# Rotated-heads stage of a decoder kernel written anew: sums of squares, projected means and mixing in small tiles of the matmul array

## Chip, cores and metric

One core of one Trainium2 chip (trn2) runs the whole program. The metric is the device time of one execution in microseconds (us), the median of the runs shown.

## What is computed

The program computes two decoder layers on x (32 items of 100 rows by 256) and a context of 361 rows by 192 per item. Each layer is attention, cross attention and a mixture of experts. The stage in question is the self attention of the second layer, "rotated heads":

```python
Q, K, V = (x @ w + b).reshape(Bn, Sn, 16, 16)        # heads of 16
prep = lambda t: tanh(t @ w1 + b1) @ w2 + b2          # 16 -> 256 -> 16, Q and K, every head
q1, k1 = complex(prep(Q)) @ H, complex(prep(K)) @ H   # 8 complex numbers of a head
qe, ke = real(R @ q1), real(R @ k1)                   # R works along the batch: items 0..7 alone are turned
qq, kk = sum(qe ** 2, -1), sum(ke ** 2, -1)           # (B, S, H)
s = qq[:, :, None, :] * kk[:, None, :, :]
attn = softmax(s / s, axis=2)                         # s / s is one wherever it is finite
out = (attn @ V) @ wo + bo
```

So the attention of a head is the mean of its values over the rows, times a factor that is one where s is finite. R mixes item a with item b = a + 1 for the first four pairs of items.

## The kernel before

`decoder` runs six stages one after another. `rotation_phase` (line 1916) is the fourth, and takes the items in 16 pairs. Pairs 0 to 3 (`TURNED`) are turned, the other twelve are plain. Each engine has its own program (`@block.tensor` and so on), an order written out by hand in its `run`, which is called once for each pair k. In it `before` is pair k-1, `after` k+1, `following` k+2, `third` k+3. I call one such call a step. All loops are unrolled, and engines meet by semaphores alone.

TensorE in a step: `first_layer` eight times (L2084: four matmuls of 32 rows, one in each row group of the array, 400 columns), `last_layer` four times (L2098: eight matmuls whose output has 32 partitions, in four column groups), `make_rows` (L2050, four transposes), `make_part` twice (L2057, keys and queries of the pair after), `make_mean` (L2065, values' mean of the pair after), `norms` twice (L2113: one matmul of 128x128 by 400 that writes each head's sum of squares on all its 16 partitions), `project` (L2119, four matmuls of 128x100 by 256), and, for turned pairs, `mix` twice (L2106 and L2108, real and imaginary part).

In PSUM (`g.psum`) six banks in three pairs hold first layers (`pair_banks`), one (`vec`) the last layers' output, and one (`side`) all else, in turn: rows, keys, queries, means, sums of squares, projection. So on `side` each product waits until the one ahead of it is copied out.

ScalarE takes tanh of two banks at a time (L2210, 16 in a step), copies rows, keys and queries (`keep_rows`, `keep_part`) and squares (L2215, L2218). VectorE normalises rows of the pairs to come (`combine`, `second_norm`, `stats`, `apply`), turns (`turn_by` L2337), finds the ends of the keys' sums (`ends_of_keys` L2343), and multiplies (`spans` L2350, `weigh` L2357 to L2364) on 128x400 elements. GpSimd gathers expert rows from DRAM (`gather`, L1976, four indirect DMAs for a pair), takes roots for the norms (L94, L96) and adds rows and bias (L1990 to L2003).

Just ahead of the stage TensorE is done with the stage before, and just behind it `wide_cross_phase` begins with a DMA.

## Time and profile before

| what | us |
|---|---|
| runs, median (lowest to highest) | 3473.21 (3470.78 to 3478.59) |
| profiled execution, its own time | 3493.37 |
| its span | 3491.2 |
| TensorE matmul busy, whole program | 3271.7 (94%) |
| VectorE, ScalarE, GpSimd busy | 1814.3, 1613.6, 1520.3 |
| stage in question, first gather to last addition | about 1229 to 1641 |

The profile is one execution. The time line gives start and length of each group of like instructions, and in square brackets how long the engine had been idle and who released it. A matmul in f32 shows as two MATMUL entries, so "x8" is four matmuls. In shapes such as 128*32, the weights have 128 rows and 32 columns. What a block of TensorE takes of its time is the distance from its start to the next block's start, since blocks overlap at their ends.

### The profile page before, as it was taken

The page shows a single profiled execution, that of the slowest core. Times are in us where ns is not written, and L with a number is a line of the kernel's source. Part 1 is how long each engine was busy: PE and PEld are TensorE (multiplying, and loading weights), DVE is VectorE, ACT ScalarE, POOL GpSimd, SP SyncE. Part 2 cuts the span into 40 slices and gives each one's busy share as a digit, 9 for nine tenths or more (in the row PEclk, how much of TensorE's full clock was granted, in tenths as well). Part 3 has the DMA queues.
Part 4 walks back from the last instruction along what each step waited for, and adds up shares of the span by engine and source line. Part 5 has one row for each costly group of instructions (what it writes and reads, how often), then busy time and mean ns, then how long its engine had stood idle before and what let it go on. Part 6 is the DMA issues. An engine that isn't in the chain of part 4 may idle for free. (4 is left out here: it accounts for less than half of the span.)

```text
span 3491.2 us, 70582 instructions
## 1 busy us (share of the span) xinstructions
PE 3271.7 (94%) x26268; PEld 2383.1 (68%) x26269; DVE 1814.3 (52%) x5671; ACT 1613.6 (46%) x3299; POOL 1520.3 (44%) x2061
## 2 busy tenths in 40 slices
PE   8997999988998869998999999999999999999997
PEld 6774566656776734443677777777777688999986
DVE  4665777755887545664444545454545465111123
ACT  4653666655764046775445554555555411111111
POOL 1002444434775154551566566666666554000035
PEclk9999999998998879999999999999999999999998
DMA  8501111100000630001000000000000013999952
GB/s 279 207 2 42 42 42 42 43 26 1 21 23 25 196 90 20 20 20 38 8 8 14 8 8 8 14 8 8 8 14 1 1 38 129 326 326 325 325 185 78
DMA packets 111486, 263.29 MB, mean 75 GB/s; under 512 B 24003, under 2 KB 70240, under 8 KB 95840
## 3 DMA queue, kind: packets, MB, share of 16 engines
q1 hardware_dynamic: 90208, 224.70, 20.1%
q0 software_dynamic: 16384, 26.29, 2.7%
q10 hardware_dynamic: 4608, 8.39, 0.6%
q8 instruction: 191, 3.13, 0.4%
q14 instruction: 95, 0.78, 0.1%
HBM read 196.61 MB, written 62.65 MB: 74 GB/s over the span
## 5 line engine op out<-in xcount | busy, mean ns | idle before, releaser
L2546 POOL TENSOR_SCALAR wide_probs<-wide_probs,wide_inverse 100x361 f32<-100x361 f32 x512 | 603.9, 1192 | 0.1
L2813 ACT ACTIVATE wide_probs<-wide_probs,wide_least 100x361 f32<-100x361 f32 x512 | 300.9, 592 | 8.6 <-DVE wide_least L2910 8.6
L2910 DVE CUSTOM_DVE_ANT_0 wide_probs<-banks,wide_bias 100x361 f32<-100x361 f32 x512 | 251.6, 529 | 45.1 <-issue 40.0
L2598 PE MATMUL banks<-w_wide_v,wide_c 64*120 64x512 f32 (+1 forms) x1152 | 266.4, 591 | 0.9 <-DVE wide_v L2896 0.9
L2592 PE MATMUL banks<-wide_c,w_wide_k 64*128 64x361 f32 x1536 | 257.4, 467 | 7.4 <-DMA wide_c<-in_ctxT 7.4
L2210 ACT ACTIVATE rot_h<-banks,w_rot_b 128x800 f32<-128x800 f32 x256 | 223.6, 924 | 86.2 <-PE banks L2084 81.1
L2544 POOL TENSOR_TENSOR wide_hold_pool<-eps 100x1 f32<-100x1 f32 x256 | 49.4, 193 | 455.1 <-DVE wide_inverse L2916 455.1
L3354 ACT ACTIVATE tiles_hT<-banks 128x512 f32<-128x512 f32 x114 | 68.1, 597 | 347.8 <-PE banks L3270 347.8
L3270 PEld LDWEIGHTS banks<-tiles_xT,tiles_w 128*128 128x128 f32 x1824 | 214.1, 193 | 4.5 <-issue 1.6
L2592 PEld LDWEIGHTS banks<-wide_c,w_wide_k 64*128 64x128 f32 x1536 | 150.5, 189 | 96.6 <-issue 10.5
L2625 PE MATMUL banks<-wide_kT,wide_qT 64*100 64x361 f32 x1024 | 208.4, 478 | 8.3 <-DVE wide_least L2910 6.6
L3270 PE MATMUL banks<-tiles_xT,tiles_w 128*128 128x128 f32 x1824 | 214.6, 276 | 1.2 <-DVE tiles_xT L3516 1.2
L3283 PE MATMUL banks<-tiles_w,tiles_hT 128*128 128x256 f32 x912 | 206.4, 379 | 0.3 <-issue 0.3
L3192 POOL TENSOR_TENSOR combine_hold<-eps 100x1 f32<-100x1 f32 x32 | 7.6, 236 | 442.0 <-DMA slots<-tiles_out 431.9
L2598 PEld LDWEIGHTS banks<-w_wide_v,wide_c 64*120 64x120 f32 (+1 forms) x1152 | 120.7, 180 | 107.1 <-issue 93.3
L3283 PEld LDWEIGHTS banks<-tiles_w,tiles_hT 128*128 128x128 f32 x912 | 168.8, 190 | 21.1 <-issue 0.4
L2643 PEld LDWEIGHTS banks<-ident,wide_probs 100*120 100x120 f32 (+1 forms) x1536 | 142.5, 140 | 31.2 <-issue 29.3
L2643 PE MATMUL banks<-ident,wide_probs 100*120 100x100 f32 (+1 forms) x1536 | 158.8, 254 | 3.0 <-ACT wide_probsT L2819 3.0
L2807 ACT COPY wide_v<-banks 120x512 f32<-120x512 f32 (+1 forms) x96 | 56.2, 585 | 223.7 <-PE banks L2598 223.7
L2804 ACT COPY wide_kT<-banks 128x361 f32<-128x361 f32 x128 | 59.0, 461 | 205.7 <-PE banks L2592 205.7
L2920 DVE COPY wide_probsT<-banks 121x400 f32<-121x400 f32 x128 | 72.9, 570 | 151.2 <-PE banks L2643 151.2
L2655 PE MATMUL banks<-wide_probsT,wide_v 120*64 120x100 f32 (+1 forms) x3072 | 148.9, 253 | 0.1
(469 smaller groups left out, 7378.6 us busy)
## 6 DMA issues: line engine op xcount, KB each, us to landing
tiles_w<-in_moe_w SPq DMA_DIRECT2D x114, 1024.0 KB, 5.1
slots<-zeros SPq DMA_DIRECT2D x58, 512.0 KB, 5.7
cross_c<-in_ctxT SPq DMA_DIRECT2D x32, 270.8 KB, 4.4
wide_c<-in_ctxT SPq DMA_DIRECT2D x32, 270.8 KB, 4.0
mix_kT<-slots SPq DMA_DIRECT2D x32, 256.0 KB, 4.2
slots<-mix_m_tiles_out ACTq DMA_DIRECT2D x32, 256.0 KB, 4.0
tiles_rows<-slots SPq DMA_DIRECT2D x57, 128.0 KB, 4.7
slots<-tiles_out SPq DMA_DIRECT2D x57, 128.0 KB, 4.9
```

The source lines that it names most:

```text
L2210: nc.scalar.activation(t.h[:, u % 2, m, 2 * half:2 * half + 2, :], pair_banks(i), ACT.Tanh, bias=w.b1[:, m:m + 1]).then_inc(h_done[i], 1)
L2546: last = nc.gpsimd.tensor_scalar(t.probs[:, i, j, :], t.probs[:, i, j, :], t.inverse[:, i, j:j + 1], None, ALU.mult)
L2592: last = nc.tensor.matmul(make_bank(unit, lane)[:, 0:CTX], w.k[rows_of(lane), k, at:at + P], t.c[rows_of(lane), of.buf, k, :], start=(k == ...
L2598: last = nc.tensor.matmul(make_bank(unit, lane)[0:kw, :], t.c[rows_of(lane), of.buf, k, k0:k0 + kw], w.v[rows_of(lane), k, of.hf * BANK:(o ...
L2625: last = nc.tensor.matmul(scores(j), t.qT[rows_of(j), here.hf, m, lane, :], t.kT[rows_of(j), here.hf, m, lane, :], start=True, stop=True)
L2643: last = nc.tensor.transpose(turned(bank)[0:cols, at], t.probs[:, i, j, k0:k0 + cols], g.ident[0:S, 0:S])
L2655: last = nc.tensor.matmul(out[rows_of(j), :], t.v[0:kw, of.hf, k, LANE_OF(i), at:at + WD], t.probsT[0:kw, group % STEP_GROUPS, bank, cols] ...
L2813: last = nc.scalar.activation(t.probs[:, i, j, :], t.probs[:, i, j, :], ACT.Exp, bias=t.least[:, i, j:j + 1], scale=-1.0, accum_out=t.rows ...
L2910: last = nc.vector.tensor_tensor_reduce(t.probs[:, i, j, :], scores(j), t.bias[:, :], -1.0, LARGEST, ALU.add, ALU.min, t.least[:, i, j:j + 1])
L2920: nc.vector.tensor_copy(t.probsT[:, group % STEP_GROUPS, 0, :], turned(0)[0:TMAX, 0:TURN_COLS]).then_inc(b[group].probsT_dve, 1)
L3270: last = nc.tensor.matmul(out_, t.w1[:, lane, c, m * P:(m + 1) * P], t.xT[:, lane, c, :], start=(c == 0), stop=(c == DC - 1))
L3283: last = nc.tensor.matmul(tile_out, t.hT[:, lane, m, :], t.w2[:, lane, m, :], start=(m == 0), stop=(m == HM - 1))
```

## The change

The whole of `rotation_phase` is written anew. `norms` makes four matmuls with 32 output partitions each, one for each lane (item of the pair) and half of the heads, in the four column groups of the array; each head then has 4 rows of 100, and VectorE works on 128x100 in place of 128x400. `mix` packs the eight real rows of each head, and makes matmuls with 64 output partitions. The mean of the values is spread over masked weights (`masked`) and projected ahead (`make_projected`, four matmuls with 32 output partitions by 256 columns, copied by VectorE to `rows`). `project` then multiplies the factors (`least`) with these rows: two matmuls of 64 rows, into two banks (`side`, `vec`) for plain pairs, or one behind the other for pairs 0 to 3. `headsT` and `mean_sum` are gone. The mean has columns 400 to 403 of `side` to itself. On GpSimd, gathers read `slot_i` itself, wait for no copy, and stand ahead of the additions; rows of pair 1 are added by VectorE. Tanh's table is loaded ahead of the first pair.

```diff
-                nc.tensor.matmul(side[:, 0:COLS], t.sum8[:, :], t.squares[:, part, :], start=True, stop=True).then_inc(ready, 1)
+                for lane in range(LANES):
+                    for c in range(DC):
+                        group = lane * DC + c
+                        last = nc.tensor.matmul(out[group * GROUP_ROWS:(group + 1) * GROUP_ROWS, :], sums(lane, c), rows(lane, c), start=True, stop=True)
...
-                nc.tensor.matmul(side[:, 0:COLS], t.real[:, :], t.by_cos[:, :], start=True, stop=False)
+                for c in range(DC):
+                    nc.tensor.matmul(side[c * MIXED:(c + 1) * MIXED, 0:LANES * S], t.real[:, :], by_chunk(t.by_cos)[:, c, :], start=True, stop=False)
...
+            def make_projected(p):
+                pe.wait_ge(s.masked, p + 1)
+                for group in range(LANES * DC):
+                    last = nc.tensor.matmul(rows_out[group * GROUP_ROWS:(group + 1) * GROUP_ROWS, :], t.masked[:, group, :, :].rearrange("p h r -> p (h r)"), w.proj[:, group % DC, :], start=True, stop=True)
...
-                for lane in range(LANES):
-                    for c in range(DC):
-                        last = nc.tensor.matmul(by_lane(side)[:, lane, :], t.headsT[:, c, lane, :], w.proj[:, c, :], start=(c == 0), stop=(c == DC - 1))
+                pe.wait_ge(s.ratio, p + 1)
+                pe.wait_ge(s.rows, p + 1)
+                half = P // LANES
+                if two_banks(p):
+                    for lane, out in ((0, side), (1, vec)):
+                        last = nc.tensor.matmul(out[0:S, 0:D], t.least[lane * half:(lane + 1) * half, :], t.rows[lane * half:(lane + 1) * half, :], start=True, stop=True)
+                    last.then_inc(s.proj_ready, 1)
+                else:
+                    nc.tensor.matmul(by_lane(side)[:, 0, :], t.least[0:half, :], t.rows[0:half, :], start=True, stop=True).then_inc(s.lane_ready, 1)
+                    pe.wait_ge(s.lane_ready, p + 1)
+                    nc.tensor.matmul(by_lane(side)[:, 1, :], t.least[half:P, :], t.rows[half:P, :], start=True, stop=True).then_inc(s.proj_ready, 1)
...
+                nc.vector.tensor_scalar(t.least[:, :], query_norms(p), t.k_least[:, :], None, ALU.mult)
+                nc.vector.tensor_scalar(t.most[:, :], query_norms(p), t.k_most[:, :], None, ALU.mult).then_inc(s.spans, 1)
```

TensorE, part of a plain step, from `project` of pair k-1 on, before:

```order
L2119 MATMUL banks<-w_rot_proj,rot_headsT 100x256 x4
L2098 MATMUL banks<-rot_h,rot_w 32x400 x8
L2084 MATMUL banks<-rot_q,rot_w 128x400 x4
L2065 MATMUL banks<-rot_ybar,w_rot_qkv 128x2 x4
L2084 MATMUL banks<-rot_q,rot_w 128x400 x4
L2113 MATMUL banks<-rot_squares,rot_sum 128x400
L2098 MATMUL banks<-rot_h,rot_w 32x400 x8
L2084 MATMUL banks<-rot_q,rot_w 128x400 x4
L2113 MATMUL banks<-rot_squares,rot_sum 128x400
```

TensorE, the like part now, from the second last layer on (L2122 is `make_projected`, L2131 `project`, L2115 `norms`, L2051 `make_part`):

```order
L2094 MATMUL banks<-rot_h,rot_w 32x400 x8
L2122 MATMUL banks<-w_rot_proj,rot_masked 32x256 x4
L2078 MATMUL banks<-rot_q,rot_w 128x400 x4
L2131 MATMUL banks<-rot_rows,rot_least 100x256 x2
L2078 MATMUL banks<-rot_q,rot_w 128x400 x4
L2094 MATMUL banks<-rot_h,rot_w 32x400 x8
L2115 MATMUL banks<-rot_squares,rot_sum 32x100 x4
L2078 MATMUL banks<-rot_q,rot_w 128x400 x4
L2051 MATMUL banks<-rot_yT,w_rot_qkv 128x200 x4
```

The blocks with 32 output partitions that are new stand right behind a last layer, which has the same shape of tile. The queries' product has moved to the place behind the keys' sums, and the mean's product, not shown, to the start of the step, a pair later than before.

GpSimd, one step before (roots of the two norms, bias, additions of rows, gathers):

```order
L96 TENSOR_TENSOR rot_ln_rstd<-rot_ln_vareps,neg_half 100x1
L2001 TENSOR_TENSOR rot_moe_seen<-eps 100x1
L2003 TENSOR_TENSOR x<-x,w_rot_proj_b 100x256 x2
L1990 TENSOR_TENSOR rot_moe_sum<-rot_moe_sum,w_mix_ln_w 100x256 x2
L1993 TENSOR_TENSOR rot_moe_sum<-rot_moe_sum,w_mix_ln_b 100x256 x2
L1997 TENSOR_TENSOR x<-x,rot_moe_sum 100x256 x2
L1973 TENSOR_TENSOR rot_moe_hold<-eps 100x1
L1976 DMA rot_moe_got<-slots,rot_gather_i 100x256 x4
```

And now:

```order
L96 TENSOR_TENSOR rot_ln_rstd<-rot_ln_vareps,neg_half 100x1
L1978 DMA rot_moe_got<-slots,mix_slot_i 100x256 x4
L1988 TENSOR_TENSOR rot_moe_sum<-rot_moe_sum,w_mix_ln_w 100x256 x2
L1991 TENSOR_TENSOR rot_moe_sum<-rot_moe_sum,w_mix_ln_b 100x256 x2
L1994 TENSOR_TENSOR x<-x,rot_moe_sum 100x256 x2
L94 TENSOR_TENSOR rot_ln_vareps<-rot_ln_meanvar,eps 100x1
L96 TENSOR_TENSOR rot_ln_rstd<-rot_ln_vareps,neg_half 100x1
```

The gathers have moved ahead of the additions, between the roots of the one norm and those of the other, and both norms of a pair are now done in one step.

## Rows read from the trace of the kernel before

**Rows 1.** The page, busy time by engine, whole program

```profile
PE 3271.7 (94%) x26268; PEld 2383.1 (68%) x26269; DVE 1814.3 (52%) x5671; ACT 1613.6 (46%) x3299; POOL 1520.3 (44%) x2061
```

**Rows 2.** Windows: steps 2, 4, 5 to 14, and last step with its tail

```profile
core 0: us, PE busy (x) PEld busy (x) DVE busy (x) ACT busy (x) POOL busy (x), PEclk, DMA share, GB/s
...
1312.77:1339.69 26.92, 24.62 (x184) 12.04 (x180) 15.64 (x37) 16.62 (x23) 12.92 (x23) 1.00 0.06 15
...
1366.63:1391.27 24.64, 23.01 (x178) 11.02 (x174) 14.56 (x36) 16.34 (x23) 11.26 (x21) 1.00 0.04 11
1391.27:1610.56 219.29, 214.49 (x1684) 100.39 (x1680) 132.26 (x309) 168.23 (x231) 118.07 (x203) 1.00 0.07 18
1610.56:1641.00 30.44, 20.64 (x146) 8.05 (x138) 13.98 (x20) 12.51 (x16) 0.00 (x0) 0.89 0.00 1
```

**Rows 3.** Time line of TensorE in a plain step: start, length, line, tiles

```profile
1572.72 0.95 PE L2084 MATMUL banks<-rot_q,rot_w 32*128 32x400 f32 x8
1573.61 1.62 PE L2057 MATMUL banks<-rot_yT,w_rot_qkv 128*128 128x200 f32 x8
...
1580.94 1.97 PE L2119 MATMUL banks<-w_rot_proj,rot_headsT 128*100 128x256 f32 x8
1582.84 1.55 PE L2098 MATMUL banks<-rot_h,rot_w 128*32 128x400 f32 x16
1584.33 0.95 PE L2084 MATMUL banks<-rot_q,rot_w 32*128 32x400 f32 x8
...
1587.27 0.94 PE L2113 MATMUL banks<-rot_squares,rot_sum 128*128 128x400 f32 x2
1588.14 1.55 PE L2098 MATMUL banks<-rot_h,rot_w 128*32 128x400 f32 x16
```

**Rows 4.** Time line of TensorE in a turned step: mixing and its waits

```profile
1315.48 0.91 PE L2106 MATMUL banks<-rot_by_cos,rot_real 128*128 128x400 f32 x2 [0.88 <-DVE rot_by_sin L2337]
...
1317.66 0.94 PE L2113 MATMUL banks<-rot_squares,rot_sum 128*128 128x400 f32 x2 [0.59 <-ACT rot_squares L2215]
```

**Rows 5.** Time line of TensorE, self attention: 16 small matmuls, then next block

```profile
130.76 0.88 PE L274 MATMUL banks<-self_probsT,self_v 100*17 100x100 f32 x32
131.57 1.62 PE L218 MATMUL banks<-self_yT,w_self_qkv 128*128 128x200 f32 x8
```

**Rows 6.** Groups by line, whole program: matmuls with 64 output partitions

```profile
L2655 PE MATMUL banks<-wide_probsT,wide_v 120*64 120x100 f32 x2048 | 132.9, 250 | 0.0
```

**Rows 7.** Groups by line, plain steps: busy us, mean ns, then idle before

```profile
L1976 POOL DMA_INDIRECT rot_moe_got<-slots,rot_gather_i x34 | 35.0, 1031 | 9.4 <-issue 9.4
L96 POOL TENSOR_TENSOR rot_ln_rstd<-rot_ln_vareps,neg_half 100x1 f32<-100x1 f32 x38 | 22.2, 584 | 3.0
L1997 POOL TENSOR_TENSOR x<-x,rot_moe_sum 100x256 f32<-100x256 f32 x18 | 12.6, 722 | 0.0
L2304 DVE SCALAR_TENSOR_TENSOR rot_moe_sum<-rot_moe_got,mix_coef,mix_x 100x256 f32<-100x256 f32 x18 | 7.9, 478 | 0.0
L2357 DVE RECIPROCAL rot_inverse<-rot_least 128x400 f32<-128x400 f32 x10 | 26.4, 2645 | 0.0
```

**Rows 8.** Time line of TensorE at the stage's start

```profile
1261.78 1.72 PE L2084 MATMUL banks<-rot_q,rot_w 32*128 32x400 f32 x8 [1.11 <-ACT rot_h L2210]
...
1269.08 0.95 PE L2084 MATMUL banks<-rot_q,rot_w 32*128 32x400 f32 x8
...
1286.72 0.95 PE L2084 MATMUL banks<-rot_q,rot_w 32*128 32x400 f32 x8
```

**Rows 9.** Time line of the last step and its tail

```profile
1611.44 0.95 PE L2084 MATMUL banks<-rot_q,rot_w 32*128 32x400 f32 x8
...
1631.88 2.65 DVE L2357 RECIPROCAL rot_inverse<-rot_least 128x400 f32<-128x400 f32 x1
...
1636.51 3.70 PE L2119 MATMUL banks<-w_rot_proj,rot_headsT 128*100 128x256 f32 x8 [5.76 <-DVE rot_headsT L2364]
1640.25 0.75 DVE L2371 TENSOR_TENSOR x<-x,banks 100x256 f32<-100x256 f32 x2 [3.89 <-PE banks L2119]
```

More of the change, by code:

```diff
@@ L2101, in last_layer @@
                     last.then_inc(vectors_ready[part], 1)
-            def mix(pr, part):
-                pe.wait_ge(turned[part], pr[2])
-                nc.tensor.matmul(side[:, 0:COLS], t.real[:, :], t.by_cos[:, :], start=True, stop=False)
-                for lane in range(LANES):
-                    last = nc.tensor.matmul(by_both(side)[:, :, lane, :], t.imag[:, :], by_both(t.by_sin)[:, :, 1 - lane, :], start=False, stop=(lane == LANES - 1))
-                last.then_inc(mixed_ready[part], 1)
@@ L2183, in _ @@
+            make_rows(0)
+            make_part(0, 1, s.k_ready)
+            first_layer(0, 0)
+            make_part(0, 0, s.q_ready)
+            first_layer(0, 1)
+            for k in range(PAIRS):
+                step(k)
+            pe.wait_ge(s.rows, PAIRS)
+            norms(LAST_PAIR, 0, query_norms(LAST_PAIR), s.qn_ready)
             pe.wait_ge(s.spans, PAIRS)
-            project(LAST)
+            project(LAST_PAIR)
         @block.scalar
@@ L2243, in _ @@
-            keep_part(FIRST, 1, s.k_ready, s.k_kept)
-            keep_part(FIRST, 0, s.q_ready, s.q_kept)
-            for k in range(2):
-                tanh(FIRST, k)
-            pairs(act, run)
+                if not is_turned(k):
+                    square(k, 0)
+            keep_rows(0)
+            keep_part(0, 1, s.k_ready, s.k_kept)
+            tanh(0, 0)
+            keep_part(0, 0, s.q_ready, s.q_kept)
+            tanh(0, 1)
+            for k in range(PAIRS):
+                step(k)
@@ new lines, in step @@
+            def step(k):
+                before, after, following = k - 1, k + 1, k + 2
+                late = not two_banks(before)
+                if is_turned(before):
+                    turn_by(before, 0)
+                if before >= 0 and is_pair(following):
+                    combine(following)
+                if before >= 0:
+                    keep_mean(before)
+                if is_pair(after):
+                    add_rows_up(after)
+                if before >= 0 and not is_turned(before):
@@ L2408, in _ @@
-            for lane, b, n in FIRST[3]:
-                dve.wait_ge(s.out_shifted, n)
-                nc.vector.tensor_tensor(g.x[:, b, :], g.x[:, b, :], v.sum[:, 0, lane, :], ALU.add).then_inc(s.stored, 1)
-            stats(FIRST)
-            copy_slots(THIRD)
-            apply(FIRST)
-            combine(SECOND)
-            add_rows_up(FIRST)
-            second_norm(SECOND)
-            keep_mean(FIRST)
-            pairs(dve, run)
-            if LAST[4]:
-                turn_by(LAST, 0)
@@ new lines, in step @@
+                if before >= 0 and not late:
+                    add(before)
+                if not is_turned(k):
+                    ends_of_keys(k)
+                if is_pair(following):
+                    stats(following)
+                if before >= 0 and late:
+                    add(before)
+                if is_pair(following):
+                    apply(following)
+                if is_turned(k):
+                    ends_of_keys(k)
+            combine(0)
+            second_norm(0)
@@ L2431 @@
+            add_rows(0)
+            stats(0)
+            combine(1)
+            apply(0)
+            second_norm(1)
+            add_rows(1)
+            add_rows_up(0)
+            stats(1)
+            apply(1)
+            for k in range(PAIRS):
+                step(k)
+            keep_mean(LAST_PAIR)
+            keep_projected(LAST_PAIR)
+            spans(LAST_PAIR)
+            weigh(LAST_PAIR)
+            add(LAST_PAIR)
 WIDE_TILES = [(0, 121), (121, 120), (241, 120)]
```

577 lines of the change are left out of this document (305 added, 272 removed).

## The prediction

> **What bounds the kernel now.** I read the page first: TensorE's matmuls are busy 94% of the span, the other engines half of it [rows 1]. So what a change in this stage is worth is read from TensorE. Then the windows, one for each kind of step. Steps 5 to 14 (plain pair behind plain pair) take 219.29 us, 21.93 each, and TensorE is busy for 214.49 of them: 0.48 us idle in a step. A turned step takes 26.92 with 2.3 idle, step 4 takes 24.64, the last one with its tail some 30 [rows 2]. ScalarE is busy 168.23 of the 219.29, 16.8 a step. It and VectorE bind only where a wait falls badly. Then the time line, for the price of each block as the distance to the next start: first layer 0.89, keys or queries 1.62 with the overlap at the end, `project` 1.90, last layer 1.49, `norms` 0.87 [rows 3]. The granted clock is 1.00, the higher level, in all these steps.
>
> **Prices of the new blocks.** None of them is in the trace, so I draw a line through blocks that use the array in tiles. A last layer is eight matmuls over four column groups, four passes of 400 columns one behind the other in a group (each f32 matmul is two entries): 1600 columns in 1.49 us. A first layer is 800 columns in 0.89 [rows 3]. So a column costs (1.49-0.89)/800 = 0.75 ns and a block 0.29 us beside. The 16 small matmuls of the self attention are eight passes of 100 columns in a group, 800 columns in 0.81 us [rows 5], where the line says 0.89; this shows that small tiles in one bank do run side by side. I take 0.24 for the fixed part, between 0.21 and 0.29.
> - `norms`: four column groups, two passes of 100: 0.15+0.24 = 0.39, for 0.87.
> - `make_projected`: two passes of 256: 0.38+0.24 = 0.63. New.
> - `project` of plain pairs: two row groups, two banks, again two passes of 256: 0.63, for 1.90. For pairs 0 to 3 one lane waits for the other: 2 x 0.55 = 1.1.
> - `mix`: two column groups. An entry of 64 output partitions by 100 columns costs 132.9/2048 = 0.065 us [rows 6]; eight of these and four of double length make 1.04, say 1.1. Before it was 1317.66-1315.48-0.59 = 1.59 [rows 4].
>
> Bounds: the least is the slope alone, 0.15, 0.38 and 0.38. The most is one tile after another at the full-array rate (0.24 us for 256 columns by `project`'s row, and not under 0.12 for a short one, half of that): `norms` 0.98, `make_projected` 1.90, `project` 1.1, `mix` 1.8. The values taken lie near the lower end because rows 5 is the nearest shape by far.
>
> Here a rule of the Trainium skill speaks against small tiles (TensorEngine Tiling, Key Properties): a change of tiling mode drains the engine. If that drain is the fixed part, `norms` and `make_projected` of a plain step, all directly behind a last layer with the same tile shape, would pay nothing, and the three would cost 0.68 and not 1.41. The trace has no two unlike blocks of one mode in a row, so it does not decide; my sum charges the fixed part everywhere.
>
> **A plain step.** Removed: 2 x 0.87 + 1.90 = 3.64. Added: 2 x 0.39 + 0.63 + 0.63 = 2.04. TensorE's work falls from 21.45 to 19.85 us. Waits: what must come back from VectorE in time is each a short hop. I set the blocks one behind another by these prices. Behind the queries' sums VectorE has one first layer's time (0.89) for two products of 100 columns; behind `make_projected` the copy has 0.89; behind the keys' sums the two ends have 0.89. Each hop needs some 0.55 to 0.65 beyond the block's end, so 0.3 is spare. The tanh behind `project` comes 0.5 us late, since TensorE now does less between two first layers. With 0.1 more elsewhere the idle time is 0.6, for 0.48. So a step takes 20.45, and **ten steps give 10 x 1.5 = 15 us**. VectorE's savings (the reciprocal of 2.65 us [rows 7] becomes a quarter of that) are off the path here. ScalarE at 16.8 in 20.4 is no bound.
>
> **Turned steps.** In steps 2 and 3 removed work is 3.64 + 2 x 1.59 = 6.8, added 0.78+0.63+1.1+2.2 = 4.7. Of 2.3 us idle [rows 2], which were TensorE waiting for VectorE's turning and ScalarE's squares [rows 4], nearly all goes, as a first layer or more stands now between. 26.9 becomes 22.5: 2 x 4.4 = 8.8, I take 8.6. Step 4 has one mix of the two: 24.64 becomes 21.6, 3.0.
>
> **The start.** GpSimd issues gathers 0.9 us sooner (it waits for no copy), but VectorE now combines pair 1 ahead of normalising pair 0, so rows reach TensorE some 1.6 us later. The first tanh then comes sooner, between keys and queries and with its table loaded, which wins 1.3 back. I book 0.3 as lost at the first projected step. Step 0 took 1286.72-1261.78 = 24.9 [rows 8]. By the sum of blocks it is 19.9, to which I add 3 for the lower clock (a first layer entry took 1.72 us there and 0.95 from 1269.08 on [rows 8]): 2.1 less than before. Step 1 is where time is lost. VectorE combines pair 2 only when the rows of pair 1 are out, and the keys' ends of pair 0 stand behind stats and apply of pair 2. That chain is 0.5 + 2.7 (combine, statistics) + 1.6 (GpSimd's roots: 2 x 0.58 and small ones) + 5.2 (four gathers, (35.0+9.4)/34 = 1.31 each) + 4.2 (additions, 6 x 0.70) + 1.0 + 1.9 + 0.8 = 17.9 us [rows 7]. It begins 2.4 us behind the start of these rows' transposes (their copy waits for two tanh) and so ends at 20.3; TensorE has 15.2 us of blocks in that time (six first layers, three last layers, keys, queries, one mix, `norms`, transposes) and stands idle some 5 us at the start of step 1. So that step is 27.2 (0.3 more than before). A stop of this length may also lower the clock. Behind the 5.76 us stop of the tail `project` took 3.70, not 1.97 [rows 9, 3]. I add 2.0, some 4 us of blocks at half speed, between 0 and 8 (the whole of step 1 low would be about 10).
> Sum to step 4: 0.3 - 2.1 + 0.3 + 2.0 - 8.6 - 3.0 = **-11.1**.
>
> **The tail.** From the last step's first layer at 1611.44 to the last addition at 1641.0 it is 29.6 us [rows 9]. The last step itself loses 1.5 as others do, and the reciprocal and three more full-width products on the critical path, some 4.4, become about 1.3. `project` falls from 3.70 to 0.6 to 1.3, but the pair's mean and `make_projected` (1.8) are added. I come to 23: **-6.5**. The next stage begins with a DMA and has the same idle time ahead of it.
>
> **The sum.** -15 - 11.1 - 6.5 = -32.6, call it 33: the profiled execution would go from 3493.4 to 3460. It lies 20 us over the median of the runs; the same 33 off the median, 3473.2, gives **3440**. A measurement of this kernel tells about 0.2%, 7 us, from no change.
>
> **Rivals.**
> - Cheaper joins: the fixed part is not paid behind a last layer. Three blocks of a plain step save 0.24 each; over 16 pairs about 11 us: 3429. For it: the self attention's block lies 0.08 under the line. Against: no like pair of blocks. This is what the drain rule would give.
> - Late hops: the spare 0.3 us behind sums, copy or ends is not there, since VectorE's small operations have a floor that the 400-wide rows do not show. With one miss of 1.2 us in each plain step and some in the turned ones, 15 are given back: 3455.
> - The clock stays low after the stop in step 1, or falls again, and pairs 1 to 2 run at half speed: 9 more, 3449.
> - GpSimd's chain: with gathers ahead of additions, the loop from combine to the next combine is 2.7+1.6+5.2+4.2+1.0+1.6+0.5 = 16.8, under 20.4. Only if it grows past that (gathers at 2.2 us each) does it bind; then the gain is about nothing: 3472.
> - Slower: small tiles whose output lies in one bank run one after another. Then `norms`, `make_projected` and `project` take 4.96 for the 3.64 removed; plain steps lose 0.9 to 1.3, turned ones gain nothing, the stop stays, the tail gains little: about +9, 3482. It decides from the point where the four blocks take more than 3.64 together. Against it: the self attention's block [rows 5].
> - The saving is made in this stage and given back at once by the next (its clock, its loads): 3473.
>
> **How the numbers follow.** Forecast 0.55, cheaper joins 0.13, late hops 0.12, clock 0.06, slower 0.06, GpSimd's chain 0.04, given back 0.04. Faster by over 0.2%: 0.55+0.13+0.12+0.06 = 0.86, and 0.03 of the last two with a small gain: 0.89. Same 0.05, slower 0.06. The range takes in cheaper joins and late hops and the bounds of the fixed part and of the clock term: 3424 to 3462. Outside lie the chain, the slower case, the return, and the ends of the others, under 0.2.
>
> **What would show it.** Plain steps at 20.3 to 20.6 between the ends of keys; `norms` to the next start under 0.45; `make_projected` and `project` near 0.63; steps 2 and 3 near 22.5; a stop of about 5 us of TensorE ahead of `make_mean` in step 1; the tail near 23. I am wrong if TensorE has more than 1 us idle in a plain step, if these blocks take over 1 us, or if the stage's end does not move.

## The result and the profile of the changed kernel

The kernel before took 3471.99 us in the median of 4 runs, the changed one 3420.82 (3419.55 to 3424.39, 4 runs): a ratio of 0.9851, 95% interval 0.9834 to 0.9868. That is 51 us; three later pairs of runs give 44 to 49. The forecast said 33, with 3424 as the near end of its range. The direction was right and the size too small. The changed kernel's profiled execution took 3419.55 us with a span of 3417.7.

The page's busy row answers to [rows 1]:

```profile
PE 3215.5 (94%) x26572; PEld 2360.8 (69%) x26573; DVE 1763.1 (52%) x5662; ACT 1611.5 (47%) x3300; POOL 1517.1 (44%) x2022
```

TensorE has 56 us less work in more instructions and is still 94% busy: it binds as before, and the program lost nearly as much time as TensorE lost work. The windows answer to [rows 2]; they are step 1, steps 2 and 3, step 4, steps 5 to 14, and the last step with its tail:

```profile
core 0: us, PE busy (x) PEld busy (x) DVE busy (x) ACT busy (x) POOL busy (x), PEclk, DMA share, GB/s
1280.42:1310.35 29.93, 23.87 (x213) 12.02 (x209) 13.33 (x42) 16.53 (x24) 18.32 (x30) 0.89 0.05 15
1310.35:1353.42 43.07, 42.48 (x421) 21.30 (x417) 25.70 (x70) 32.84 (x47) 25.84 (x41) 1.00 0.07 20
1353.42:1374.42 21.00, 20.48 (x201) 10.02 (x198) 14.11 (x37) 16.40 (x24) 12.76 (x21) 1.00 0.08 21
1374.42:1571.61 197.19, 190.06 (x1844) 91.47 (x1840) 95.98 (x292) 166.00 (x231) 113.35 (x177) 1.00 0.07 18
1571.61:1593.77 22.16, 16.42 (x180) 7.30 (x176) 7.39 (x22) 12.42 (x16) 0.00 (x0) 0.98 0.00 1
```

Both profiled executions begin the stage at 1228.8 us. It ended with the last addition at 1641.0 before (1640.25 + 0.75, [rows 9]) and at 1593.8 now: 47.3 less. Piece by piece, in us:

```
piece                         before    after   change   forecast
start to first layer of step 0  33.0     32.2     -0.8     +0.3
step 0                          24.9     19.5     -5.5     -2.1
step 1                          26.9     29.9     +3.0     +2.3 (0.3 and 2.0 for the clock)
steps 2 and 3                   53.9     43.1    -10.8     -8.6
step 4                          24.6     21.0     -3.6     -3.0
steps 5 to 14                  219.3    197.2    -22.1    -15
last step and tail              29.6     22.2     -7.4     -6.5
sum                                              -47.3    -32.6
```

One piece has the wrong sign (the start, by 1.1 us) and step 1 lost slightly more than forecast; every other gain was undersized. TensorE's time line in a plain step shows where, beside [rows 3]:

```profile
1461.42 1.55 PE L2094 MATMUL banks<-rot_h,rot_w 128*32 128x400 f32 x16
1462.78 0.61 PE L2122 MATMUL banks<-w_rot_proj,rot_masked 128*32 128x256 f32 x8
1463.33 0.95 PE L2078 MATMUL banks<-rot_q,rot_w 32*128 32x400 f32 x8
1464.21 0.68 PE L2131 MATMUL banks<-rot_rows,rot_least 64*100 64x256 f32 x4
1465.39 0.95 PE L2078 MATMUL banks<-rot_q,rot_w 32*128 32x400 f32 x8 [0.50 <-ACT rot_h L2252]
...
1471.53 1.55 PE L2094 MATMUL banks<-rot_h,rot_w 128*32 128x400 f32 x16
1473.01 0.95 PE L2078 MATMUL banks<-rot_q,rot_w 32*128 32x400 f32 x8
...
1476.16 1.55 PE L2094 MATMUL banks<-rot_h,rot_w 128*32 128x400 f32 x16
1477.53 0.35 PE L2115 MATMUL banks<-rot_squares,rot_sum 128*32 128x100 f32 x8
1477.82 0.95 PE L2078 MATMUL banks<-rot_q,rot_w 32*128 32x400 f32 x8
```

The reader is to take the distance from one start to the next, not the length in the second column. A last layer (L2094) takes 1.48 us where a first layer follows (1471.53 to 1473.01) and 1.36 to 1.37 where `make_projected` or `norms` follows (1461.42 to 1462.78, 1476.16 to 1477.53). `norms` itself takes 0.29 and `make_projected` 0.55.

At the start and in step 1, beside [rows 8]:

```profile
1256.27 2.71 PE L2051 MATMUL banks<-rot_yT,w_rot_qkv 128*128 128x200 f32 x8
1258.91 0.95 PE L2078 MATMUL banks<-rot_q,rot_w 32*128 32x400 f32 x8
...
1287.14 1.87 PE L2059 MATMUL banks<-rot_ybar,w_rot_qkv 128*128 128x2 f32 x8 [5.77 <-DVE rot_k_least L2427]
```

A first layer takes 0.95 us already at 1258.91; it did so from 1269.08 before [rows 8]. And the forecast stop is there: 5.77 us idle ahead of `make_mean`, then 1.87 for a block that takes 1.05 at the higher clock. The tail, beside [rows 9]:

```profile
1589.80 0.38 PE L2115 MATMUL banks<-rot_squares,rot_sum 128*32 128x100 f32 x8 [0.55 <-DVE rot_rows L2414]
1592.31 0.68 PE L2131 MATMUL banks<-rot_rows,rot_least 64*100 64x256 f32 x4 [2.13 <-issue]
...
1593.02 0.75 DVE L2450 TENSOR_TENSOR x<-x,banks 100x256 f32<-100x256 f32 x2 [0.82 <-PE banks L2131]
```

TensorE waits 2.13 us there, where it waited 5.76. The profile names no releaser, but VectorE's short chain, which `project` needs, runs in that time and ends at 1592.2. `project` is down from 3.70 (at the lower clock; 1.97 at the higher one) to 0.68.

### The profile page after: what moved, and what is told of

Read it like the earlier page. It is cut to its first block and busy times, and to the rows that moved or that the text cites. A ratio compares the mean times of both kernels' runs of the same rounds, so it can differ in the third digit from the quotient of the medians.

```text
span 3417.7 us, 71219 instructions
## 1 busy us (share of the span) xinstructions
PE 3215.5 (94%) x26572; PEld 2360.8 (69%) x26573; DVE 1763.1 (52%) x5662; ACT 1611.5 (47%) x3300; POOL 1517.1 (44%) x2022
## 5 line engine op out<-in xcount | busy, mean ns | idle before, releaser
L3367 PEld LDWEIGHTS banks<-tiles_w,tiles_hT 128*128 128x128 f32 x912 | 168.8, 190 | 21.1 <-issue 0.4
```

The source lines that it names most:

```text
L3367: last = nc.tensor.matmul(tile_out, t.hT[:, lane, m, :], t.w2[:, lane, m, :], start=(m == 0), stop=(m == HM - 1))
```

## The experiments

Executions of one kernel begin this stage anywhere from 1223.6 to 1232.1 us, which is the stages ahead of it and most of the spread of a run. So beside times I give the **stage length**: from VectorE's copy into `rot_fold_b` to its first write of `wide_y` in the next stage. It is 418.3 and 418.6 us in two profiles of the kernel before and 371.1, 370.8, 370.8 and 370.7 in four of the changed one: 47.6 us of gain, with a spread of 0.4.

**The changed kernel again**, three times on three chips.

> The changed kernel again, as the bar for the runs beside it. Both theories: within 0.1% of 3420.8 us. Open in it: whether the granted clock comes back at about 1258 us again (it was 1268.5 in the kernel before), whether step 0 takes 19.5 us again, and whether the stage that follows is again some 3 us shorter than in the kernel before.

> The changed kernel once more. In the three last experiments plain steps took 20.6 to 21.4 us up to step 12 and 0.9 to 1.5 less in steps 13 and 14, even where the edit touched no step at all (the blocks appended at the end): VectorE began the first span 0.82 us behind the start of the queries' sums there, 0.42 in the profile of the changed kernel. If that is the changed kernel itself on another chip, this run shows either 19.72 in every plain step and 0.985 of the kernel before, or 20.64 up to step 12 and 0.990. If the edits caused it, it shows 19.72.

> The changed kernel again, as the bar for the runs beside it: plain steps of 19.72 and 0.985 to 0.987 of the kernel before on a chip like the first, 20.64 up to step 12 and 0.990 on one like the second.

Measured: 3422.19, 3417.44 and 3422.41 us, ratios 0.9869 (0.9851 to 0.9887), 0.986 (0.9835 to 0.9884) and 0.9872 (0.9854 to 0.9891). Plain steps take 19.72 in all. Step 0 takes 19.45 again in two of them and 21.1 in the first: there the granted clock came back 5 us behind TensorE's return and fell again for 3.4 us inside step 0, while the piece ahead of the step was 1.8 us shorter. So these two pieces are to be read together; their sum is 51.3 to 51.6 in all four profiles of the changed kernel. From the first `wide_y` to VectorE's last `wide_probs` it takes 1132.1 to 1136.8 here, 1132.6 in the first profile of the changed kernel, and 1137.0 and 1135.0 in the kernel before: the 3 to 4 us that seemed to be won in the next stage lie in the spread of executions and are not the change's.

**The kernel before again.**

> The kernel before as one of the experiments, for a second profile of it beside those of the changed kernel. If the 10.7 us by which the higher clock came back sooner at the start belong to the change, it stays low here until about 1268 us of a stage that starts at 1228.8, and step 0 takes 24.9 us again; if that was one execution's luck, it comes back by 1260 and step 0 takes 22 to 23. The last stage took 112 us in the kernel before's profiled execution and 89 in the changed one's: 89 here if that was the execution, 112 if the change shortened it.

Measured: ratio 0.9996, stage 418.6, step 0 again 24.9 us. The granted clock:

```profile
1255.00:1260.00 5.00, 5.00 (x24) 0.50 0.28 58
1260.00:1265.00 5.00, 3.01 (x16) 0.50 1.01 396
1265.00:1270.00 5.00, 4.79 (x32) 0.63 0.96 195
```

So the late return of the clock belongs to the kernel before: 21 us behind TensorE's return from its wait in both profiles, against 5 to 10 in all those of the changed one. The last stage is a different matter: from the last `wide_probs` to the end it is 683 us here and 707 in the profile shown ahead of the prediction, 683 to 687 in the changed kernel. That profile's time, 20 us over the median, is not the kernel's, as the prediction's choice to subtract from the median assumed. It is most likely its chip's: on one of the chips below, on which the kernel before took 3491 us, all four profiles have 704 to 711 us there, and no other profile has more than 687.

**Only the tile shape undone, for the sums of squares**: each group's weights are padded with zeros to 128 columns, and the groups add up.

```diff
-out[group * GROUP_ROWS:(group + 1) * GROUP_ROWS, :], sums(lane, c), rows(lane, c), start=True, stop=True
+out, sums(lane, c), rows(lane, c), start=(group == 0), stop=(group == LANES * DC - 1) 
```

> Both sums of squares of a pair as four accumulating matmuls over the full array (weights padded with zeros), the rest as changed. Theory of the joins: a block behind one of the same tile shape starts 0.12 to 0.26 us sooner, so here the last layer ahead of the sums takes 1.48 us again for 1.365, and the sums 0.87 for 0.29: 0.70 for each, 1.4 in a plain step (21.1 for 19.72), in all about 3443. Theory of short blocks: the last layer stays at 1.365, only the sums grow, 1.16 in a plain step (20.9), about 3439.

Measured: 3446.07 us, 23.9 over the changed kernel beside it (ratio to the kernel before 0.9943, 0.9927 to 0.996), stage 395.6, plain steps 21.22. The time line of TensorE in one of these steps:

```profile
1466.63 1.55 PE L2094 MATMUL banks<-rot_h,rot_w 128*32 128x400 f32 x16
1468.11 1.14 PE L2115 MATMUL banks<-rot_squares,rot_sum 128*128 128x100 f32 x8
1469.17 0.95 PE L2078 MATMUL banks<-rot_q,rot_w 32*128 32x400 f32 x8
...
1472.49 1.55 PE L2094 MATMUL banks<-rot_h,rot_w 128*32 128x400 f32 x16
1473.86 0.61 PE L2122 MATMUL banks<-w_rot_proj,rot_masked 128*32 128x256 f32 x8
```

The last layer ahead of the full-array sums takes 1.48 again, the one ahead of the still small `make_projected` 1.37. The work of the last layer is the same; what follows it sets its price, as the theory of the joins says. I call a **join** what a block takes longer because its neighbour has another tile shape.

**Sums, projected means and mixing all over the full array**, the new order kept (weights padded as above, `start` and `stop` set so that the groups add up).

> As the last, and the projected mean rows and the mixing over the full array too. Theory of the joins: 1.4 + (1.90 - 0.55) + 0.12 = 2.9 in a plain step, 22.6, longer than the kernel before's 21.93; with the turned pairs about 3421 + 46 = 3467, so that nearly the whole gain was in the tile shape and not in the other order of the work. Short blocks: last layers at 1.365, 22.2, about 3460. If the other order of the work (fewer and better hidden waits) carries the gain, under 3450.

Measured: 3477.21 us, ratio 1.0029 (1.0013 to 1.0045): slower than the kernel before. Plain steps take 22.71, steps 2 and 3 26.40, the stage 424.7 where it was 418.5. So without the small tiles the rest of the rewrite is 6 us slower than the kernel before: the whole gain hangs on the tile shape of these blocks. What the new order is worth by itself is not shown, since this version also carries the padded `make_projected` (1.93 us), which the kernel before does not have. Both expected times were too low. The full-array sums take 1.06 us, in eight short entries, and not 0.87, of which the plain steps give back a part as waits that go (21.22 and 22.71 for 21.1 and 22.6). Most of the 10 us missing in this run lie in the steps with mixing: it takes 1.74 us over the full array for 0.83, twice, and steps 2 and 3 take 4.9 us more each.

**Blocks behind themselves and in turn**, appended behind the stage's last block, profiled once.

```diff
+for row in ([F], [L], [F, L], [N], [F, N], [L, N], [J], [L, J], [X], [L, X], [R], [F, R], [C], [F, C], [L, C], [M], [F, M], [L, N, F], [L, J, F]):
+    for n in range(8):
+        for block_of in row:
+            block_of(n)
```

F is a first layer, L a last layer, N the sums, J `make_projected`, X the mixing, R `project`, C keys, M the means.

> Behind the stage's last block some 330 more blocks run on TensorE with no waits among them: each kind eight times behind itself, then eight times in turn with a first or a last layer. Nothing is computed with them. Theory of the joins: a pair of unlike blocks takes 0.24 to 0.5 us more in turn than the two take each behind itself (first and last layer, last layer and sums in unlike row tiles), and a last layer followed by sums or projected rows, the same column tiles, nothing more. Theory of short blocks: turn and row differ by under 0.05 us for every pair.

Time line of TensorE in it; a row with x128 or x64 is eight blocks of a kind without a break, and the first row is three first layers (x24) out of a row of eight:

```profile
1609.96 2.19 PE L2242 MATMUL banks<-rot_q,rot_w 32*128 32x400 f32 x24
1611.97 0.85 PE L2242 MATMUL banks<-rot_q,rot_w 32*128 32x400 f32 x8
...
1612.76 10.95 PE L2247 MATMUL banks<-rot_h,rot_w 128*32 128x400 f32 x128
1623.64 0.95 PE L2242 MATMUL banks<-rot_q,rot_w 32*128 32x400 f32 x8
...
1642.45 1.56 PE L2251 MATMUL banks<-rot_squares,rot_sum 128*32 128x100 f32 x64
1643.93 0.95 PE L2242 MATMUL banks<-rot_q,rot_w 32*128 32x400 f32 x8
...
1653.37 1.53 PE L2247 MATMUL banks<-rot_h,rot_w 128*32 128x400 f32 x16
1654.71 0.35 PE L2251 MATMUL banks<-rot_squares,rot_sum 128*32 128x100 f32 x8
1654.88 1.53 PE L2247 MATMUL banks<-rot_h,rot_w 128*32 128x400 f32 x16
```

Eight last layers take 1623.64 - 1612.76 = 10.88; the last is followed by a first layer and takes 1.49 (as [rows 3] show), so one behind another takes (10.88 - 1.49)/7 = 1.34. Between two blocks of sums it also takes 1.34 (1653.37 to 1654.71); between a first layer and the sums, as in the kernel, 1.37. The row of first layers needs care: the granted clock is at its lower level from 1605.9 to 1609.3, so only its second half counts:

```profile
1606.00:1609.00 3.00, 3.00 (x24) 0.50 0.00 0
1610.00:1612.70 2.70, 2.70 (x36) 1.00 0.02 6
```

There three first layers take 1611.97 - 1609.96 = 2.01, or 0.67 each. In us to the next block's start, all at the higher clock:

```
block                    before its own kind   before another shape   join
last layer                       1.34                 1.48            0.14
norms                            0.17                 0.31            0.14
make_projected                   0.43                 0.55            0.11
project                          0.43                 0.61            0.18
mixing                           0.68                 0.83            0.15
keys or queries                  1.35                 1.55            0.20
first layer                      0.67                 0.88            0.21
```

(The joins are taken before rounding. `make_projected` has a last layer ahead of it here, so its join is that of one side.) Every kind pays: 0.14 to 0.21 us among blocks of other tile shapes, the first layer most. A last layer and sums or projected rows in the same column tiles join for nothing. A pair of unlike blocks in turn takes 0.29 (last layer and mixing) to 0.41 us (first layer and keys) more than the two behind themselves, 0.35 for first and last layer: the 0.24 to 0.5 expected. "Under 0.05" held for no pair of unlike shapes. With the joins taken off, a last layer's 1600 columns and a first layer's 800 both cost 0.84 ns a column, and so do the sums' 200: 0.17.

**Each kind where nothing beside it has its shape**, profiled once.

```diff
-for row in ([F], [L], ...
+for row in ([F, C], [F, N, C], [F, J, C], [F, R, C], [F, X, C], [F, L, C], [F, M, C], [F, T, C], [F, M, T, F, C], [T], [C], [M], [C], [N], [C]):
```

> More blocks behind the end, each kind in turn between a first layer and the keys' block over the full array, where nothing beside it has its shape. From the first such run: leaving column tiles or the full array for another shape costs 0.11 to 0.20 us, leaving row tiles nothing. Then the sums cost 0.31 us here, projected rows 0.54, project 0.60, mixing 0.83, the means 0.9, transposes 0.5, and the keys' block 1.55 everywhere. Theory of short blocks: the same as each behind itself (0.17, 0.43, 0.43, 0.68). Last the means' block (matmuls of 2 columns) eight times between keys' blocks: the granted clock falls in it again, if it was these matmuls and not the chip.

Measured: sums 0.31, `make_projected` 0.57, `project` 0.61, mixing 0.83, means 0.91 and transposes 0.40, as each costs with its join; only the transposes are off the 0.5 expected. The keys' block takes 1.55 behind most and 1.53 behind the means; behind the transposes it takes 1.47, which I did not expect. (The 0.57 of `make_projected` has a join on both sides, 0.14.) The clock fell in the narrow blocks again; the last section shows it.

**The queries' sums twice**, once joined and once apart (`spare` makes the same four matmuls into unused columns).

```diff
                     else:
+                        spare(before)
                         norms(before, 0, query_norms(before), s.qn_ready)
```

> In plain steps the queries' sums of squares run twice, the first time into spare columns, both right behind the last layer. Theory of the joins: two passes of 100 columns and nothing for the join, 0.15 to 0.17 us a step, 12 steps, 2 us in all. Theory of short blocks: the whole 0.29 again, 3.5 us in all.

```diff
                         pe.wait_ge(s.spans, before + 1)
+                        spare(before)
                     make_part(after, 1, s.k_ready)
```

> The same second sums, but between the first layer behind them and the keys of the pair that follows, blocks of two other tile shapes. Theory of the joins: 0.15 for the passes and 0.25 for one more join, 0.4 a step, 4.8 us in all, 2.8 more than where they were joined. Theory of short blocks: 0.29 a step, 3.5 us in all, as where they were joined.

The time line of TensorE in step 14, joined:

```profile
1569.80 0.35 PE L2124 MATMUL banks<-rot_squares,rot_sum 128*32 128x100 f32 x8
1569.97 0.35 PE L2115 MATMUL banks<-rot_squares,rot_sum 128*32 128x100 f32 x8
1570.25 0.95 PE L2078 MATMUL banks<-rot_q,rot_w 32*128 32x400 f32 x8
```

And apart:

```profile
1569.01 0.95 PE L2078 MATMUL banks<-rot_q,rot_w 32*128 32x400 f32 x8
1569.90 0.38 PE L2124 MATMUL banks<-rot_squares,rot_sum 128*32 128x100 f32 x8
1570.21 1.62 PE L2051 MATMUL banks<-rot_yT,w_rot_qkv 128*128 128x200 f32 x8
```

The same block costs 0.17 us joined and 0.31 apart; steps 13 and 14 take 19.89 and 20.03 for 19.72. This is the join again, 0.14, in the kernel itself. Joined it is as the theory said (0.15 to 0.17), apart less (0.4 expected); a block as such, 0.29 in both places, is refuted. The times of the two runs, 3461.62 and 3460.70 (ratios 0.9911 and 0.9913), say nothing on it, because of what comes next.

**Late hops on one chip.** These two, the first bench and the run with another order at the start (below) shared a chip on which the kernel before took 3491.07 us. Their steps 5 to 12 were longer than the edit explains: 20.64 us in the first bench, whose steps are those of the changed kernel, and 19.72 again in steps 13 and 14. VectorE's first span (`rot_least`), here in the changed kernel and then in the run with another start, whose plain steps are the same, on this chip:

```profile
1497.67 0.32 DVE L2432 TENSOR_SCALAR rot_least<-banks,rot_k_least 128x100 f32<-128x100 f32 x1 [0.75 <-PE banks L2115]
```

```profile
1488.25 0.32 DVE L2433 TENSOR_SCALAR rot_least<-banks,rot_k_least 128x100 f32<-128x100 f32 x1 [1.15 <-PE banks L2115]
```

The sums began at 1497.25 in the one and at 1487.43 in the other: VectorE starts 0.42 us behind them, or 0.82. That puts the keys' block 0.2 late, the tanh behind it and so on, 0.92 us in a step and some 11.5 us over the stage. It is the rival "late hops", at one place, on one chip of five; there a plain step even fails the prediction's own sign, under 1 us idle. It happens only in steps in which GpSimd issues gathers at that moment, so I moved them.

```diff
-                if is_pair(k + 3):
-                    gather(k + 3)
                 if is_pair(k + 2):
                     add_rows(k + 2)
+                if is_pair(k + 3):
+                    gather(k + 3)
+                if is_pair(k + 2):
                     roots(m1, k + 2)
```

> GpSimd issues the four gathers of a step behind its additions and not ahead of them, so none is issued while VectorE waits for the queries' sums. If the issue of a gather delays VectorE's start there, the first span begins 0.42 us behind the sums on any chip and plain steps take 19.72: 0 us where they take 19.72 already (or 0.5 a step more, where the gathers land too late for the next sum of rows), 11 us less where they take 20.64. If something else sets the delay, the steps stay as they are beside it.

> The gathers behind the additions, again, in the hope of a chip where plain steps take 20.64: there 19.72, 11 us less, if the issue of the gathers delays VectorE behind the queries' sums, and 20.64 if not. On a chip where they take 19.72: the same as the changed kernel or up to 2 us more, for the longer step 1.

Measured: 3424.57 and 3422.50 us (0.9867, 0.9844 to 0.989; 0.9874, 0.9857 to 0.9892), beside 3417.44 and 3422.41 for the changed kernel; stage 371.0 and 370.5. Neither ran on the chip with the late hops, so these say only that moving the gathers costs nothing elsewhere. Whether their issue is the cause stays open.

**The stop of step 1 taken away.**

```diff
+                if before < 0:
+                    combine(following)
+                    turn_by(k, 1)
                 if is_pair(after):
                     add_rows_up(after)
                 if before >= 0 and not is_turned(before):
                     spans(before)
                     weigh(before)
-                if before < 0:
-                    combine(following)
-                    turn_by(k, 1)
```

> VectorE combines pair 2 in step 0 ahead of adding up the rows of pair 1. If the 5.8 us stop of TensorE in step 1 and the low clock behind it come from that chain alone, the stop goes, the clock stays at its higher level, and steps 0 and 1 together take about 41 us for 49.4: 8 us faster than the changed kernel, about 3413. If the clock falls for another reason, or GpSimd's gathers set the stop (the rows of pair 2 late whatever VectorE does), 0 to 3 us are won.

> Pair 2 combined in step 0, again: it won 9.6 us where it ran beside the changed kernel, but with the gathers moved as well only 4 against its own bar. If the stop of step 1 is what it wins, 8 to 10 us under the changed kernel again; if part of that was the spread of the runs, 3 to 6.

Measured: 3412.61 and 3413.63 us, 9.6 and 8.8 under the changed kernel beside them; ratios to the kernel before 0.985 (0.9833 to 0.9868) and 0.9843 (0.9829 to 0.9856). Stage 362.5 and 362.8, 8.2 less. TensorE in step 1:

```profile
1278.39 0.95 PE L2078 MATMUL banks<-rot_q,rot_w 32*128 32x400 f32 x8
1279.27 1.05 PE L2059 MATMUL banks<-rot_ybar,w_rot_qkv 128*128 128x2 f32 x8
```

`make_mean` follows without a wait, at the higher clock. 5.8 us of stop and 2.4 of lower clock were the price of VectorE combining pair 2 behind `add_rows_up(1)`, which had to wait for the copy of pair 1's rows. This is the best version that ran.

**Both together.**

> The gathers behind the additions and pair 2 combined in step 0 together. The stop of step 1 goes again: 9 to 10 us under the run with the gathers behind alone. This is the best version if both hold.

Measured: 3420.44 us beside 3417.44, stage 367.7. The expectation failed: only 3.1 us of the stage are won for 8.2. With the gathers behind the additions the stop ahead of `make_mean` in step 1 is 4.8 us for 5.8, and with pair 2 combined sooner as well it is 3.2, but it does not go. The two edits should not be combined.

**The start: order, and the two-column block.**

```diff
             make_part(0, 1, s.k_ready)
-            first_layer(0, 0)
+            pe.wait_ge(s.k_kept, 1)
             make_part(0, 0, s.q_ready)
+            first_layer(0, 0)
             first_layer(0, 1)
...
```

ScalarE's copies and tanh change places in the same way.

> The start as in the kernel before: keys and queries of pair 0 first, then the two first layers, with their tanh behind both copies. If the first layer between them is what brought the higher clock 10.7 us sooner (1257.8 for 1268.5 us), step 0 takes some 3 to 5 us more, about 3424 to 3426. If the clock's return does not hang on that order, 0 to 1.5 us more.

Measured on the chip with the late hops: 3458.12 us (0.9903, 0.9888 to 0.9918). Counted to the first ends of keys, 60.0 us for 57.7 in the bench on the same chip: the order is worth 2.3. The clock came back by 1260 us in both and dipped again, here for longer (0.65 and 0.67 in the two windows to 1270, for 0.66 and 1.00). So the order is not what held it down for 21 us before. The next two runs put a two-column block at the start of the changed kernel, and took it from there in the kernel before.

```diff
             make_part(0, 1, s.k_ready)
             first_layer(0, 0)
+            for m in range(DC):
+                for c in range(DC):
+                    nc.tensor.matmul(mean_out[:, m * LANES:(m + 1) * LANES], w.qkv[:, c, 2 * D + m * P:2 * D + (m + 1) * P], t.yT[:, c, :, 0],
+                                     start=(c == 0), stop=(c == DC - 1))
             make_part(0, 0, s.q_ready)
```

> The changed kernel with eight matmuls of two columns more, in the form of the means' block, between the first first layer and the queries of pair 0 (their results are overwritten later). In the kernel before such a block stood at this place and the clock came back at 1268 to 1269 us, 21 us behind TensorE's return from its wait; without it 5 to 9.5 us behind. In the bench twice eight such blocks in a row lowered the clock. If the narrow block is what holds the clock down, it comes back some 15 to 20 us behind the return, and the stage takes 4 to 6 us more than 370.8. If not, it comes back as before and the stage takes 1 to 2 us more.

Measured, in 2 runs: 3429.90 us (0.9884, 0.9856 to 0.9913), stage 376.7, 5.9 more than without. TensorE:

```profile
1259.18 1.87 PE L2231 MATMUL banks<-rot_yT,w_rot_qkv 128*128 128x2 f32 x8
1260.91 3.02 PE L2051 MATMUL banks<-rot_yT,w_rot_qkv 128*128 128x200 f32 x8
1263.86 1.52 PE L2078 MATMUL banks<-rot_q,rot_w 32*128 32x400 f32 x8
```

The clock comes back some 13 us behind TensorE's return, not 15 to 20 as I had written, and falls once more for 3.4 us in step 0. Of the 5.9 us, 4.4 lie ahead of step 0's transposes: the block's own 1.7, the queries behind it wholly at the lower clock (2.95 us to the next start, for 2.4 to 2.6 in three of the four profiles without it), and the first layers and the last layer behind them, in part at the lower clock too. The other 1.5 lie in step 1, where the lower clock outlasted the stop by 8.4 us for 5 to 5.5 in the four profiles of the changed kernel; two other runs without the block (the first bench and the sums twice, joined) show that too, so these 1.5 may not be the block's.

> The kernel before with the means of pair 0 moved from between its two first first layers to behind the first last layer of step 0. If the narrow block held the clock down, the clock now comes back 5 to 10 us behind TensorE's return (by 1258) and not 21; the stage may take less than 418.5 us or, since VectorE waits for the means, more. If keys and queries behind one another or the earlier start held it down, it still comes back near 1268.

Measured: 3476.15 us (1.002, 1.0007 to 1.0033); the clock still came back 21 us behind the return. It then fell again at 1269.8 for 6.8 us, as TensorE waits 3.65 us there for VectorE, which waits for the means; the stage takes 425.7 us, 7 more. So in the kernel before the two-column block was not what held it down, although it costs clock where it is put into the changed kernel. What did is open.

## Why the prediction was right in its direction and wrong in its size

**What bounds.** Right: TensorE at 94% before and after, and each piece moved with TensorE's work.

**Prices of the new blocks: the step that failed.** The prediction drew a line through first and last layers, got a fixed part of 0.24 us for a block and charged it "everywhere". The runs show it is no fixed part of a block but a join, 0.14 to 0.21 us, paid when the tile shape changes. The line itself came out askew, since its two shapes have unlike joins (0.21 and 0.14): 0.75 ns a column and 0.29 us beside, where the bench has 0.84 ns. Three of the four new blocks of a plain step stand directly behind a last layer and share its shape, so putting one in pushes the join back without adding one. The sums then add 1.37 + 0.29 - 1.48 = 0.17 us (with rounding) where 0.39 was charged, twice; `make_projected` adds 1.36 + 0.55 - 1.48 = 0.43 for 0.63; `project`, between first layers, 0.61 for 0.63 as said. That is 0.65 us a step. The rival "cheaper joins" had this mechanism and priced it at 0.72 a step (three times 0.24) and 3429 in all. The Trainium skill's rule (TensorEngine Tiling, Key Properties: a change of tiling mode drains the array) stood in the prediction as the rule that would make the blocks cheaper; the bench agrees that a change costs, for all seven kinds, at 0.11 to 0.21 us, though no run shows that a drain is the reason. The prediction gave that rival 0.13 because "no like pair of blocks" was in the trace. The better reading was that the 0.24 is an intercept of two shapes which never follow their own kind, so it could not tell a block's cost from a join's; the rule should have weighed more than the line.

**The plain step.** Forecast 20.45, measured 19.72. The blocks are 0.65 of the 0.73. The rest is waits, which as distances from start to start are 0.79 us in a step before and 0.85 now: 0.06 more where 0.12 was booked. The page's idle time hides a part of them. It was 0.48 before, because blocks overlap at their ends: `make_mean` took 1.17 to the next start, of which 0.26 was a wait for the tanh, and 0.91 now. It is 0.72 now for the 0.6 forecast, at the two places named (0.50 of it behind `project` for the tanh). Over ten steps the miss is 7.1 us of the 14.7.

**Turned steps.** 21.54 each for the 22.5 forecast: the mixing takes 0.83 for the 1.1 charged, twice, the sums as above, and `project` in two parts 1.33 for 1.1. Step 4 goes the same way. 2.8 us of the miss.

**The start.** Forecast -1.8 to the end of step 0, measured -6.3. The sum of step 0 took the lower clock of [rows 8] to last as long as before ("3 for the lower clock"). It ended sooner: 9.3 us behind TensorE's return for 21, and ahead of step 0, so that where 3 us were booked there were none. Step 0 was mis-sized by 3.4 with it, and the start itself by 1.1. That the sooner return belongs to the change is shown (two profiles of the kernel before at 21, all four of the changed one at 5 to 10); its cause is not.

**Step 1.** The chain of VectorE and GpSimd was right, link by link: a stop of "some 5 us" at the start of step 1, 5.77 measured, and a clock term of 2.0, 2.4 measured by taking the stop away. 29.9 us for 29.2.

**The tail.** 22.2 for 23: right but for the cheaper blocks.

**The rivals.** Small tiles one after another (3482) is refuted by 0.17 us for sums behind sums. Late hops (3455) did not happen on four chips and did on the fifth, at 11.5 us. The clock that stays low for pairs 1 to 2 did not come: it was back 5 to 5.5 us behind the stop in the changed kernel, and 8.4 at most in the other runs, which costs 1.5. GpSimd's chain never bound: it waits some 5 us in each plain step for VectorE. The gain was not given back behind the stage.

## What to carry to other kernels

Price a block on TensorE by the distance to the next start, and by what follows it: a change of tile shape costs 0.11 to 0.21 us here, so put blocks of one shape behind one another, and pad no small reduction up to the full array (doing so here costs 54 us of stage length, the whole gain and 6 more). An intercept fitted through blocks that never follow their own kind is not a property of the block, and a row of blocks gives a price only where the granted clock stays at one level. Measure a stage by its own length inside the profiles (spread 0.4 us) before arguing from run times (spread 10 us), and profile the kernel before twice.

## What the runs showed of the hardware that I had not expected

**The clock of a busy TensorE fell in blocks of two-column matmuls.** In the first bench the engine is never idle here, yet (windows of TensorE: length, busy, granted clock, DMA):

```profile
1734.00:1777.00 43.00, 43.00 (x318) 1.00 0.00 1
1777.00:1781.00 4.00, 4.00 (x32) 0.87 0.00 0
1789.00:1816.00 27.00, 27.00 (x127) 0.50 0.00 1
1822.00:1850.00 28.00, 28.00 (x348) 1.00 0.01 2
```

From 1777.6 the means' block runs eight times behind itself, and at 1779.9 the clock falls to the lower level, 1.2 GHz. It stays there for another 27 us while the same block alternates with first layers, and comes back when last layers and sums follow. In the second bench eight such blocks between keys' blocks lowered it again (0.89, then 0.54 in windows of 6 us) and it was back at 1.00 in the window after. There, alternated with first layers and keys from the higher clock, they did not lower it. One such block at a place where the clock is still low costs 4.4 us ahead of step 0 for its 1.7 (one profile).

**Chips differ at one hop.** The same program has VectorE start 0.42 us behind the sums on four chips and 0.82 on a fifth, only while gathers are issued, with every instruction there as long as elsewhere but the normalisations that run beside the gathers (0.48 us in the mean for 0.41). On that chip 3458 us for 3491 is what the change gained, with the other start's 2.3 us in it.
